# Gates of the first two groups scanned and split in PSUM, early bank users dealt anew, and a new order of all steps

## What is computed

```
x = x + tanh(g_xattn) * mlstm(layernorm(x), ctx, ctx)
x = x + tanh(g_ffn)  * ffn(layernorm(x))
# mlstm, per batch, 8 heads of 32 channels:
ig, fg = gates([q, k, v]);  cs = cumsum(log_sigmoid(fg))
log_D = tril(cs[:, None] - cs[None, :]) + ig[None, :]
D = exp(log_D - rowmax(log_D));  C = (q k^T / sqrt(32)) * D
h = (C / (max(|sum C|, exp(-rowmax)) + eps)) v;  out = layernorm(h) * ln_scale
# ffn: z = x W_fc^T (256 to 1024), y = relu(z)^2 W_proj^T, out = spikes of 5 steps / 5
```

## Time and profile before

| what | us |
|---|---|
| median of 3 runs (lowest, highest) | 625.95 (625.66, 629.16) |
| the profiled execution | 626.91 |
| its span in the trace | 625.1 |
| PE, DVE, POOL, ACT busy | 576.2, 535.9, 496.6, 485.2 |

### The profile page before, as it was taken

One profiled execution on the slowest core, in us unless ns is written; L12 is line 12 of the kernel. 1 busy time (PEld: TensorE's weight loads), 2 busy tenths in 40 slices (PEclk: granted clock), 3 DMA queues, 4 the chain that ended last, 5 costly groups with the idle time before them and its releaser, 6 DMA issues.

```text
span 625.1 us, 17746 instructions
## 1 busy us (share of the span) xinstructions
PE 576.2 (92%) x6032; PEld 477.3 (76%) x6032; DVE 535.9 (86%) x1292; ACT 485.2 (78%) x1012; POOL 496.6 (79%) x541
## 2 busy tenths in 40 slices
PE   0466989999999999999999999999999999999995
PEld 0265888887888788887888788887788787887895
DVE  4898899979989898989989898989989888877454
ACT  4665888878888778887888788887888768776673
POOL 3988889897896879888896879888796878865542
PEclk9995899999999999999999999999999999999999
DMA  8764646664576336761675336852574427600002
GB/s 277 161 136 110 138 112 123 144 124 112 106 170 138 102 89 116 176 154 57 117 164 129 102 90 120 189 136 57 113 151 113 103 56 120 139 18 23 12 2 68
DMA packets 73193, 71.34 MB, mean 114 GB/s; under 512 B 8720, under 2 KB 68752, under 8 KB 73104
## 3 DMA queue, kind: packets, MB, share of 16 engines
q1 hardware_dynamic: 71888, 70.00, 49.2%
q10 hardware_dynamic: 1216, 0.21, 0.3%
HBM read 27.44 MB, written 8.39 MB: 57 GB/s over the span
## 4 chain that ended last, share of the span: by engine, by line
PE 81%; DVE 10%; ACT 3%; issue 2%; DMA 1%; ACTq 0%; DVEq 0%
PE z_ps L1033 28%; PE y_ps L1101 25%; PE qk_ps L739 4%; PE misc_ps L484 4%; PE arg_ps L724 4%; PE misc_ps L550 2%; PE pv_ps L788 2%; PE pv_ps L786 2%; PE pv_ps L787 2%; PE pv_ps L863 2%; DVE spikes L1119 1%; DVE decay L758 1%; PE y_ps L1130 1%; PE qk_ps L1101 1%; PE arg_ps L1101 1%
## 5 line engine op out<-in xcount | busy, mean ns | idle before, releaser
L768 POOL TENSOR_TENSOR c_lo<-decay 128x512 bf16<-128x512 f32 x128 | 133.1, 1049 | 52.9 <-DVE decay L758 38.7
L1076 POOL TENSOR_TENSOR sq_lo<-w_raw,sq_hi 128x512 fp32r<-128x512 f32 (+1 forms) x96 | 112.1, 1172 | 24.5 <-ACT w_raw L1056 24.5
L1033 PE MATMUL z_ps<-x_hi,wfc_hi 128*128 128x512 f32 (+1 forms) x288 | 115.5, 401 | 1.5 <-ACT w_raw L1043 1.3
L1033 PE MATMUL z_ps<-x_hi,wfc_lo 128*128 128x512 f32 (+1 forms) x288 | 106.7, 370 | 0.0
L1033 PE MATMUL z_ps<-x_lo,wfc_hi 128*128 128x512 f32 (+1 forms) x288 | 106.7, 370 | 0.0
L1101 PE MATMUL y_ps<-sq_hi,wpr_hi 128*128 128x512 f32 (+1 forms) x256 | 104.0, 406 | 0.0
L1101 PE MATMUL y_ps<-sq_lo,wpr_hi 128*128 128x512 f32 (+1 forms) x256 | 97.4, 380 | 0.0
L1101 PE MATMUL y_ps<-sq_hi,wpr_lo 128*128 128x512 f32 (+1 forms) x256 | 97.4, 380 | 0.0
L750 ACT ACTIVATE decay<-arg_ps,lqk_col 128x512 f32<-128x512 f32 x128 | 86.7, 677 | 13.7 <-PE arg_ps L727 13.2
L758 DVE TENSOR_TENSOR decay<-qk_ps,decay 128x512 f32<-128x512 f32 x128 | 87.1, 681 | 7.4 <-PE qk_ps L739 6.1
L1119 DVE SCALAR_TENSOR_TENSOR spikes<-y_ps,spikes 128x1024 bf16<-128x1024 f32 (+1 forms) x64 | 73.8, 1153 | 1.2
(11 more groups left out here) (185 smaller groups left out, 1734.8 us busy)
## 6 DMA issues: line engine op xcount, KB each, us to landing
x_in<-x SPq DMA_DIRECT2D x32, 256.0 KB, 3.6
kT_in<-ctx_cols SPq DMA_DIRECT2D x32, 256.0 KB, 3.3
v_in<-ctx_rows SPq DMA_DIRECT2D x32, 256.0 KB, 3.7
k_stack<-kT_hi SPq DMA_DIRECT2D x64, 128.0 KB, 3.2
k_stack<-kT_lo SPq DMA_DIRECT2D x64, 128.0 KB, 3.6
q_stack<-qT_hi SPq DMA_DIRECT2D x64, 128.0 KB, 3.9
q_stack<-qT_lo SPq DMA_DIRECT2D x64, 128.0 KB, 4.1
out<-w_raw SPq DMA_DIRECT2D x32, 256.0 KB, 3.3
```

The lines of the kernel that those rows point to most:

```text
L768: e.tensor_tensor(c_lo[i % NCH][:, :], c, top(c), ALU.subtract).then_inc(sem("c_lo"), 1)
L1033: ins = e.matmul(z_ps[:, tokens(q)], lhsT, rhs, start=(n == 0), stop=(n == len(terms) - 1))
L1076: e.tensor_tensor(sq_lo[n % NSQ][:, tokens(q)], relu[n % NRE][:, tokens(q)], sq_hi[n % NSQ][:, tokens(q)].bitcast(fp32), ALU.subtract).the ...
```

## The change

Four things are done at once.

1. For groups 0 and 1 (`IN_PSUM = 2`) the gates stay in the PSUM bank that `gate_T` wrote. `gate_pre` does only the sum for f, in place; the sum for i moves into the subtraction after the scan, as one `scalar_tensor_tensor`. The scans, `row_max`, the two differences and the four splits read or write the bank (`am_of`). The second input of the maximum scan becomes a broadcast column `low_col`, which one more memset fills. The bank is given back by the fourth split instead of by `gate_pre`.
2. The early users get other banks: gates and floors in `z_ps`, the transposed gates of groups 0 and 2 in bank 1 and of group 1 in bank 0 of `y_ps`. The first `z_step` and the first `y_step`s wait for them.
3. All five programs have another order, in the written-out start, in the loop and at the end. `MISC_ORDER` follows it.
4. In the start of `scalar_program` `setup_tanh` moves from the place after `ln1_apply(0)` to the place after `gates_out(2)`.

```diff
+        IN_PSUM = 2
+        EARLY = {("g", b): "z" for b in range(6)} | {("fT", g): "z" for g in range(3)} \
+            | {("gT", g): ("y1", "y0")[g % 2] for g in range(3)}
...
+        def early_users_done(eng, bank):
+            for (kind, i), b in EARLY.items():
+                if b == bank and kind == "gT" and i < IN_PSUM:
+                    eng.wait_ge(sem("am_split"), 4 * i + 4)
+                elif b == bank:
+                    eng.wait_ge(sem(f"{kind}_free"), i + 1 - (IN_PSUM if kind == "gT" else 0))
+        def am_of(g):
+            if g < IN_PSUM:
+                return bank_of(("gT", g)).rearrange("p (k s) -> p k s", k=2)
+            return am[:, :, :]
...
# gate_pre
-            e.tensor_scalar(f_neg[0:r, :], pre[0:r, S:2 * S], gate_bias[0:r, 1:2], 0.0, ALU.add, ALU.min)
-            e.tensor_scalar(i_pre[0:r, :], pre[0:r, 0:S], gate_bias[0:r, 0:1], None, ALU.add).then_inc(sem("gT_free"), 1)
+            if g < IN_PSUM:
+                f = pre[0:r, S:2 * S]
+                e.tensor_scalar(f, f, gate_bias[0:r, 1:2], 0.0, ALU.add, ALU.min).then_inc(sem("gate_neg"), 1)
...
# gate_cumsum
+            f = am_of(g)[0:r, 1, :] if g < IN_PSUM else f_neg[0:r, :]
+            link(e, "vector", e.tensor_tensor_scan(cs[0:r, :], f, f_log[0:r, :], 0.0, ALU.add, ALU.subtract))
+            a = am_of(g)[0:r, 0, :]
+            if g < IN_PSUM:
+                ins = e.scalar_tensor_tensor(a, a, gate_bias[0:r, 0:1], cs[0:r, :], ALU.add, ALU.subtract)
...
# gate_cummax
+            a, m = am_of(g)[0:r, 0, :], am_of(g)[0:r, 1, :]
+            b = low_col[0:r, :].broadcast_to([r, S]) if g < IN_PSUM else a
+            link(e, "vector", e.tensor_tensor_scan(m, a, b, LOWEST, ALU.max, ALU.max))
```

The start of `scalar_program`, up to `gate_softplus(2)`, in the two orders (`ln1_rstd`, `gate_softplus`, `floor_exp`, `decay_exp` and `setup_tanh` are the steps that use a table):

```diff
-            setup_load_g(e) / setup_load_gates(e) / ln1_rstd(e, 0) / ln1_apply(e, 0) / setup_tanh(e)
-            q_hi(e, 0) / split_wfc_hi(e, 0) / ln1_apply(e, 1) / ln1_rstd(e, 1) / split_wfc_hi(e, 1)
-            gates_out(e, 0) / q_hi(e, 1) / gate_softplus(e, 0) / gates_out(e, 1) / ln1_apply(e, 2)
-            ln1_rstd(e, 2) / split_wpr_hi(e, 0) / setup_load_scale(e) / am_split(e, 0, 0) / q_hi(e, 2)
-            am_split(e, 0, 2) / load_m_rows(e, 0) / gate_softplus(e, 1) / ln1_apply(e, 3) / floor_exp(e, 0)
-            ln1_apply(e, 4) / q_hi(e, 3) / decay_exp(e, 0, 0) / am_split(e, 1, 0) / floor_exp(e, 1)
-            decay_exp(e, 0, 1) / gates_out(e, 2) / q_hi(e, 4) / decay_exp(e, 0, 2) / gates_out(e, 3)
-            am_split(e, 1, 2) / decay_exp(e, 0, 3) / load_m_rows(e, 1) / gate_softplus(e, 2)
+            setup_load_gates(e) / ln1_rstd(e, 0) / split_wfc_hi(e, 0) / ln1_apply(e, 0) / q_hi(e, 0)
+            ln1_apply(e, 1) / setup_load_g(e) / ln1_rstd(e, 1) / setup_load_scale(e) / gates_out(e, 0)
+            split_wpr_hi(e, 0) / ln1_apply(e, 2) / q_hi(e, 1) / gate_softplus(e, 0) / ln1_apply(e, 3)
+            q_hi(e, 2) / ln1_rstd(e, 2) / split_wfc_hi(e, 1) / gates_out(e, 1) / am_split(e, 0, 0)
+            floor_exp(e, 0) / am_split(e, 0, 2) / load_m_rows(e, 0) / gate_softplus(e, 1) / ln1_apply(e, 4)
+            decay_exp(e, 0, 0) / q_hi(e, 3) / decay_exp(e, 0, 1) / floor_exp(e, 1) / am_split(e, 1, 0)
+            decay_exp(e, 0, 2) / gates_out(e, 2) / setup_tanh(e) / am_split(e, 1, 2) / gates_out(e, 3)
+            q_hi(e, 4) / decay_exp(e, 0, 3) / gate_softplus(e, 2) / split_wpr_hi(e, 1) / load_m_rows(e, 1)
```

The places in the other programs that the prediction speaks of:

```diff
# vector_program, start: the steps around gate_pre(2), and around ln3_offset(0)
-            cmul(e, 0, 3) / state_own(e, 0) / gate_pre(e, 2) / gate_cumsum(e, 2) / gate_cummax(e, 2)
+            gate_pre(e, 2) / cmul(e, 0, 3) / gate_cumsum(e, 2) / gate_cummax(e, 2)
-            x1_step(e, 0) / q_lo(e, 5) / cmul(e, 1, 2) / ln3_stats(e, 0) / state_own(e, 1) / ln3_offset(e, 0) / cmul(e, 1, 3)
+            x1_step(e, 0) / cmul(e, 1, 2) / ln3_stats(e, 0) / cmul(e, 1, 3) / ln3_offset(e, 0) / q_lo(e, 5) / state_own(e, 1)
# vector_program, end
-            spikes_step(e, 16, 0..4) / out_step(e, 15) / out_step(e, 16) / spikes_step(e, 17, 0..4) / out_step(e, 17)
+            out_step(e, 15) / spikes_step(e, 16, 0..4) / spikes_step(e, 17, 0..4) / out_step(e, 16) / out_step(e, 17)
# tensor_program, start
-            inter(e, 1) / z_step(e, 0, 0) / arg(e, 2, 1) / q_T(e, 6) / arg(e, 2, 2) / qk(e, 2, 1)
+            pv(e, 1, 1) / qk(e, 2, 1) / arg(e, 2, 1) / z_step(e, 0, 0) / q_T(e, 6) / arg(e, 2, 2)
# tensor_program, end
-            y_step(e, 17, 5) / count_T(e, 16) / y_step(e, 17, 6) / y_step(e, 17, 7) / count_T(e, 17)
+            y_step(e, 17, 5) / y_step(e, 17, 6) / y_step(e, 17, 7) / count_T(e, 16) / count_T(e, 17)
# sync_program, start: the load of W_fc goes from sixth to fourth, behind load_k(0)
-            load_x(e, 2) / load_x(e, 3) / setup_load_wfc(e) / load_k(e, 1)
+            setup_load_wfc(e) / load_x(e, 2) / load_values(e, 0) / load_x(e, 3) / load_values(e, 1) / load_x(e, 4) / load_k(e, 1)
```

More of the change, by code:

```diff
@@ L305, in setup_cols @@
             e.memset(eps_col[:, :], LN_EPS)
+            e.memset(low_col[:, :], LOWEST)
             e.memset(lqk_col[:, :], LOG_QK_SCALE).then_inc(sem("cols_ready"), 1)
@@ L1092, in y_step @@
                 else:
-                    for kind, (bank, end) in EARLY.items():
-                        if bank == q:
-                            e.wait_ge(sem(f"{kind}_free"), end)
+                    early_users_done(e, f"y{q}")
             e.wait_ge(sem("square_lo"), n + 1)
@@ L1391, in scalar_program @@
+            square(e, 1, 0)
+            am_split(e, 3, 2)
+            ln3_rstd(e, 2)
+            floor_exp(e, 3)
+            relu_step(e, 1, 1)
+            ln1_rstd(e, 4)
+            ln3_apply(e, 2)
+            decay_exp(e, 3, 3)
             square(e, 1, 1)
+            relu_step(e, 1, 2)
             x2_hi_step(e, 2)
-            relu_step(e, 1, 2)
-            ln1_rstd(e, 4)
+            ln1_apply(e, 8)
             decay_exp(e, 4, 0)
             square(e, 1, 2)
-            decay_exp(e, 4, 1)
@@ L1764, in vector_program @@
             x1_step(e, 3)
+            q_lo(e, 8)
             cmul(e, 4, 3)
+            state_own(e, 4)
+            ln3_stats(e, 3)
             out_step(e, 0)
-            state_own(e, 4)
-            q_lo(e, 8)
-            ln3_stats(e, 3)
             cmul(e, 5, 0)
+            ln3_offset(e, 3)
             h_norm(e, 4)
@@ L1872, in vector_program @@
                 ln3_stats(e, 4 * n + 5)
-                ln3_offset(e, 4 * n + 5)
-                q_lo(e, 4 * n + 11)
-                h_norm(e, 4 * n + 6)
+            ln3_offset(e, 25)
+            q_lo(e, 31)
+            h_norm(e, 26)
             ln2_stats(e, 26)
@@ L1883, in vector_program @@
             ln3_stats(e, 26)
+            state_own(e, 27)
+            ln3_offset(e, 26)
             cmul(e, 27, 1)
-            ln3_offset(e, 26)
-            state_own(e, 27)
             spikes_step(e, 12, 0)
@@ L1939, in vector_program @@
             ln3_stats(e, 30)
+            state_own(e, 31)
+            ln3_offset(e, 30)
             cmul(e, 31, 1)
-            ln3_offset(e, 30)
-            state_own(e, 31)
             spikes_step(e, 14, 0)
@@ L2392, in tensor_program @@
             z_step(e, 17, 6)
+            count_T(e, 15)
             y_step(e, 17, 3)
```

784 lines of the change are left out of this document (393 added, 391 removed).

## The result

The changed kernel takes 621.92 us (median of 19 runs, 618.91 to 625.63) where the kernel before takes 629.46 us beside it (19 runs, 624.65 to 632.23): ratio 0.9907, 95% interval 0.9884 to 0.9931. The forecast was 1.7 us slower; by the ratio it is about 5.8 us faster. So the two spans, 623.5 and 625.1, understate the gain.

What follows compares the result with a forecast made beforehand. PE, busy 576.2 of 625.1 us, was taken as the bound. Start +1.6, PE's early work -0.4 and end +0.5 made +1.7 us on the median of 625.95: 627.7 us, range 621.5 to 633.0.

Steps and rivals of the forecast that it cites:

- PSUM chain (part one): Gates of groups 0 and 1 in the start: 3.0 us from scan to last difference, saving 1.9 and 2.4 us.
- Table loads (part two): ACT in the start: nine table loads instead of three, six more, 7.7 us on ACT.
- The rival without new loads: Start: ACT needs no added table loads, 5.5 us less than the forecast, 622.2 us; chance 0.15.
- The rival of more hidden idle time: Late start caught up in idle time before 100 us, and the loop loses 2.0 us of idle: 624.0 us; chance 0.15.
- (a): ACT's start: split_wfc_hi(0) waits for W_fc, ln1_apply(0) begins at about 11.9 us, ln1_apply(1) ends at 16.6 instead of 17.0.
- (b) to (g): Rest of the start: scans of groups 0, 1, 2 from 25.0, 36.4, 47.7 us; h_norm(0) 2.0 late, first z 1.6.
- `qk` and `arg`: PE does qk(2, 1) and arg(2, 1) ahead of the first z: worth up to 0.85 us, taken as 0.4.
- my start: All steps up to the first z together: it comes 1.6 us late, at 65.3 us.
- The end: out_step(16) now stands between the last spikes and out_step(17): 0.3 to 0.8 us more, taken as 0.5.
- The loop: Middle 400 us: the new order can bring 4 us at most, PE's waits being 4.1 us; nothing taken.
- The rival of a stalling loop: In the loop, a cmul or x2_lo behind a longer DVE step stops PE, 1.1 us a pass: 634.2 us; chance 0.15.

Runs made afterwards that it cites:

- a_no_psum: The changed kernel with IN_PSUM = 0, so groups 0 and 1 are scanned in SBUF, order and banks kept: ratio 0.9921 to the kernel before, 622.9 us.
- the third column: First-relu times of the changed kernel with low_col allocated last, so other tiles keep the addresses of before: ratio 0.9947 to the kernel before.
- r_before: An unchanged copy of the kernel before, for a second profile and the noise: ratio 1.001 to the kernel before.
- b_xlo_first: The kernel before with DVE's x2_lo_step moved ahead of gate_cummax in the loop: ratio 1.0308 to the kernel before.
- b_pad: The kernel before with an unused 32-byte tile that shifts later tiles to the changed kernel's addresses: ratio 1.001 to the kernel before, median 627.85 us.

## Why the prediction was wrong

**PSUM chain (part one): the durations right.** 3.0 us per group were forecast and 3.0 measured (23.56 to 26.56, 34.66 to 37.65); each difference takes 0.33 us. Of the savings, 1.9 and 2.4 us, `a_no_psum` shows 0.2 and 1.7: in the new order group 0's stretch takes only 3.16 us from SBUF as well.

**Table loads (part two): right.** Nine, at the lines named, 1283 ns each. Undoing six of them gave 4.8 us, where the rival without them had 5.5. The rival without new loads falls, although its 622.2 us is the nearest to what was measured: that is luck. The rival of more hidden idle time, 624.0, falls too, since the loop's idle time stayed.

**(a) Mis-sized.** `ln1_apply(1)` ended at 15.10 us, not 16.6. W_fc had landed when ACT came for it: `split_wfc_hi(0)` started at 9.34 us without a wait, `ln1_apply(0)` at 10.45 instead of the forecast 11.9. I had ACT free at 10.70 as before, but DVE began its statistics of x at 3.92 us, without `setup_rows` ahead of them, and the first Ln's load stood at 6.22.

**(b) to (g): the steps right up to `h_norm(0)`, with (a)'s 1.5 us carried on.** Scans of group 0 from 23.56 (forecast 25.0), of group 1 from 34.66 (36.4), of group 2 from 46.29 (47.7). `h_norm(0)` was 0.4 us late, not 2.0. PE came to the place of the first z 0.1 us late, not 1.6; z itself was 1.0 late for the 0.88 us of `qk` and `arg` that I had booked as a gain of 0.4. The relus come 0.4 us earlier in job 0, 2.0 earlier in job 1 (87.27 us, 89.28 before) and 0.5 later in job 2 (119.41, 118.95). The loss of 1.7 us by job 5 in the third column comes mostly behind that, in the stretch with the stall; that it has the size of my start, 1.6, is chance.

**The end: not shown.** From the first relu of job 17 to the end it took 21.81 us instead of 21.64, where I took 0.5 more; but kernels with the end of before take 21.57 to 21.88 there, so no cost can be told.

**The loop: this step failed.** "PE waits for 4.1 us in 400, so it can bring 4 us at most; I take nothing." The idle time stayed (4.45 us), and the stretch from job 5 to 13 became 5.4 us shorter (281.26 to 275.89; 4.3 against `r_before`, whose 280.18 holds no further wait). Two things were behind that. First, a bound from PE's idle time is none where PE's records overlap: 0.7 us of waits in each pass stood inside busy time. Second, I had the mechanism in hand: the earlier trace rows show DVE's operation held by POOL's, and I used it in the start and not in the loop, where the two scans of every pass had 1.12 and 0.98 us for what takes 0.68 elsewhere (the earlier trace rows has the 0.69). "A rotation with neighbours swapped" was no reason for nothing: whether DVE's operation starts ahead of POOL's or behind it is decided by a few hundredths of a microsecond, and costs 0.3 to 1.3 us.

**The term that was absent.** `low_col`'s 32 bytes moved the operands of z and y, 0.36 us a pass. In the forecast it appears as a memset.

**The rival of a stalling loop** named the right kind of place, DVE's queue, and the wrong sign; `b_xlo_first` shows that another order can stall so, at 2.7 to 4.8 us a pass.

**What stays open.** The stall at 127.6 us: DVE waits there for a late load of x (PE 2.8 us for the `decay` behind it), and the clock is granted at 0.53 in the seven microseconds that follow.

```profile
DVE stat L396 <- DMA x_in<-x: 3.6, 1, 3.6
...
PE qk_ps L773 <- DVE decay L792: 2.8, 1, 2.8
...
120.00:127.00 7.00, 4.79 (x70) 3.81 (x68) 3.34 (x12) 3.01 (x7) 4.50 (x6) 0.98 0.67 196
127.00:134.00 7.00, 6.43 (x28) 5.21 (x29) 5.70 (x16) 5.70 (x11) 6.33 (x7) 0.53 0.89 185
```

It is in the profiles of after, `r_before` (3.14 us), `b_pad` (3.39) and others, and not in that of before. Why the load is late in some executions wasn't tried, and so neither whether the new start makes the stall more likely. Open too is why the matmuls stream faster from the shifted addresses.

## What to carry to other kernels

Do not take PE's idle time as the bound of what a new order can bring: compare the time from one event of a pass to the same event of the next, and the distance of the starts where PE changes from one kind of work to another. Where DVE works on SBUF beside GpSimd, look at each shape's durations over the whole run; the same shape at 0.68 and 1.12, or 0.27 and 1.34, was a wait for the other engine here, and steps can be ordered (or sources put in PSUM) so that it isn't met. An ask for ACT's function set belongs early, ahead of the Ln and Exp that alternate: here it takes the changed kernel from 0.991 of the one before to 0.983, 615.83 us.

## What the runs showed of the hardware that I had not expected

- A new tile of 32 bytes changed TensorE's pace: 512-column fp32r matmuls every 0.229 us with the streamed tiles at multiples of 64 bytes (here also of 128), every 0.232 to 0.233 at odd multiples of 32, at a granted clock of 1.00.
- A scan on SBUF that starts while a POOL operation runs ends 0.50 to 0.55 us after that operation (or after the next, if that follows at once) and takes 0.98, 1.12, 1.14 or 2.58 us for 0.68. With one source in PSUM it took 0.68 or 0.69 us beside one, 18 times out of 18.
- In `b_xlo_first` a wait of 2.7 us of PE was followed by matmuls at the lower clock (0.427 us each for 0.233), which cost some 1.5 us more.
